# A third set of slots for the gathered rows of a graph attention kernel

## The reference

```python
def _gat_layer(x, src, dst, W_i, a_src_i, a_dst_i, b_i):
    h = (x @ W_i).reshape(n, H, C)              # 4 heads of 32 channels
    es = jnp.einsum('nhc,hc->nh', h, a_src_i)
    ed = jnp.einsum('nhc,hc->nh', h, a_dst_i)
    e = es[src] + ed[dst]
    e = jnp.where(e > 0, e, NEG_SLOPE * e)
    m = jax.ops.segment_max(e, dst, num_segments=n)
    p = jnp.exp(e - m[dst])
    denom = jax.ops.segment_sum(p, dst, num_segments=n)
    alpha = p / denom[dst]
    msg = alpha[:, :, None] * h[src]
    out = jax.ops.segment_sum(msg, dst, num_segments=n)
    return out.reshape(n, H * C) + b_i
```

## Time and profile before

| | us |
|---|---|
| median of 3 runs | 10176.32 |
| lowest and highest run | 10164.33, 10180.4 |
| span of the profiled execution | 10190.0 |
| POOL busy | 4949.5 (49%) |
| PE busy | 5634.0 (55%) |
| DVE busy | 5295.9 (52%) |
| ACT busy | 4630.7 (45%) |

### The profile page before, as it was taken

One profiled execution on the slowest core, in us unless ns is written; L12 is line 12 of the kernel. 1 busy time (PEld: TensorE's weight loads), 2 busy tenths in 40 slices (PEclk: granted clock), 3 DMA queues, 4 the chain that ended last, 5 costly groups with the idle time before them and its releaser, 6 DMA issues.

```text
span 10190.0 us, 128499 instructions
## 1 busy us (share of the span) xinstructions
PE 5634.0 (55%) x33883; PEld 4498.0 (44%) x33883; DVE 5295.9 (52%) x12476; ACT 4630.7 (45%) x8410; POOL 4949.5 (49%) x5153
## 2 busy tenths in 40 slices
PE   3999899735445454544454444545434444444446
PEld 2777566524444444443444444444423333333334
DVE  5888511335555555554555555555634444444445
ACT  2555200245555555553555555555434444444444
POOL 1000100356666666662566666666456666666660
PEclk9999899655555555555555555555555555555557
DMA  2333355133333333332333333333322222222221
GB/s 83 137 139 139 133 189 190 34 98 106 101 101 102 101 104 104 102 101 59 100 103 100 102 102 102 105 102 102 79 71 74 72 70 70 75 70 70 70 75 32
DMA packets 600497, 985.13 MB, mean 97 GB/s; under 512 B 330887, under 2 KB 454493, under 8 KB 560781
## 3 DMA queue, kind: packets, MB, share of 16 engines
q1 hardware_dynamic: 216924, 540.94, 15.6%
q0 software_dynamic: 163376, 356.21, 14.9%
q10 hardware_dynamic: 219648, 81.82, 3.0%
HBM read 755.78 MB, written 222.74 MB: 96 GB/s over the span
## 4 chain that ended last, share of the span: by engine, by line
PE 28%; DVE 21%; another core or an unknown queue 18%; DVEq 15%; issue 12%; POOL 3%; ACT 2%; DMA 1%; POOLq 0%; ACTq 0%; SPq 0%
PE bank L1038 12%; DVEq L1352 11%; DVE acc L1982 10%; PE bank L1264 6%; POOL arena L704 3%; DVE arena L1969 3%; PE bank L1062 2%; DVEq L1982 2%; DVE bank L1938 2%; PE bank L1192 2%; PE bank L1204 2%; DVEq L1974 1%; DVE arena L1940 1%; PE bank L1335 1%
## 5 line engine op out<-in xcount | busy, mean ns | idle before, releaser
L704 POOL DMA_INDIRECT arena<-row_table,staged_idx x4980 | 4712.4, 946 | 3140.3 <-issue 1777.7
L1264 PE MATMUL bank<-arena 128*128 128x136 f32 x9984 | 2508.6, 431 | 1638.0 <-issue 737.8
L1264 PEld LDWEIGHTS bank<-arena 128*128 128x128 f32 x9984 | 2218.6, 318 | 1813.3 <-issue 1795.4
L1982 DVE TENSOR_TENSOR acc<-acc,bank 128x136 f32 x4992 | 1476.7, 296 | 2271.3 <-remote 950.9
L861 ACT ACTIVATE pick_dist<-col,dst_local 128x128 bf16<-128x128 f32 x4992 | 1521.8, 388 | 442.9 <-remote 407.8
L1038 PE MATMUL bank<-arena 128*128 128x385 bf16 (+1 forms) x7448 | 1325.0, 327 | 36.4 <-DVE arena L1722 19.9
L813 ACT COPY x_mem<-bank 128x384 f32<-128x384 f32 x416 | 199.0, 478 | 1714.5 <-remote 1192.8
L1038 PEld LDWEIGHTS bank<-arena 128*128 128x128 bf16 x7448 | 702.0, 98 | 457.6 <-issue 21.5
L648 POOL TENSOR_TENSOR arena<-acc,node_stat 128x896 f32 x14 | 24.8, 1771 | 1672.9 <-POOLq L660 988.4
L1969 DVE TENSOR_TENSOR arena<-arena,bank 128x528 f32<-128x528 f32 x1248 | 832.3, 688 | 0.7
L1204 PE MATMUL bank<-ident,x_mem 96*128 96x96 f32 x1664 | 364.3, 374 | 764.0 <-DVE x_mem L1630 521.4
(11 more groups left out here) (371 smaller groups left out, 5508.6 us busy)
## 6 DMA issues: line engine op xcount, KB each, us to landing
arena<-dst_rows SPq DMA_DIRECT2D x156, 1024.0 KB
cell_rows<-arena SPq DMA_DIRECT2D x75, 1568.0 KB, 5.1
arena<-cell_rows SPq DMA_DIRECT2D x75, 1568.0 KB, 6.5
edge_stats<-x_mem ACTq DMA_DIRECT2D x416, 192.0 KB
arena<-row_table,staged_idx POOLq DMA_INDIRECT x4980
x_mem<-in_edge_attr SPq DMA_DIRECT2D x208, 192.0 KB
x_mem<-segment_flags SPq DMA_DIRECT2D x416, 96.0 KB
arena<-change_rows SPq DMA_DIRECT2D x312, 64.0 KB
```

What stands on the lines that cost most here:

```text
L704: pool.indirect_dma_start(gathered[:, at, :], None, table, bass.IndirectOffsetOnAxis(staged_idx[:, at:at + 1], 0)).then_inc(att_gathered[n ...
L1264: mm = pe.matmul(region(k)[:, 0:ROW], pick[:, k, :], gathered[:, b * GROUP + k, :], start=True, stop=True)
L1982: done = dve.tensor_tensor(row, row, region(m * BATCH + k), ALU.add)
```

## The change

A constant `SETS = 3` is new. The gathered rows get three sets of 32 slots. Two are the memory they had; the third is the last 32 of the 49 tiles of `H`, right before it in `arena`. Group g uses the set `(g + 1) % 3`. Groups 1, 4, ... 49 lie in `H`'s memory. POOL now waits for sums of group g - 3 and not at all for the first three groups of a layer; ACT stages three groups at the layer's start, and later, when the rows of group g + 1 have landed, those of group g + 4. After SP's last edge loads of a layer it waits for the sums of group 49 and loads tiles 17 to 48 of `H` back from the table; DVE waits for that load before it uses `H` at the layer's end. The two halves of `gathered` keep their other uses. The core of the diff:

```diff
+        OWN_KEPT = NT - GROUP
+        row_sets = arena[:, OWN_KEPT * ROW:(NT + 2 * GROUP) * ROW].rearrange("p (k w) -> p k w", w=ROW)
...
-        staged_idx = sb("staged_idx", [P, 2 * GROUP], I32)
+        staged_idx = sb("staged_idx", [P, SETS * GROUP], I32)
...
+        def row_set(g):
+            return (g + 1) % SETS
+        def set_rows(g):
+            first = (row_set(g) + 1) % SETS * GROUP
+            return row_sets[:, first:first + GROUP, :]
+        def rows_gathered(g):
+            return 16 * (g // SETS * GROUP + (LAST_REAL if g == NG - 1 else GROUP))
...
+                sp.wait_ge(att.summed, (n * NG + NG) * NBATCH)
+                sp.dma_start(H[:, OWN_KEPT:NT, :], table.rearrange("(t p) w -> p t w", p=P)[:, OWN_KEPT:NT, :]
+                             ).then_inc(n3.own_back, 16)
...
-                        pool.wait_ge(att.staged, n * (NG + 1) + it * 2 + b + 1)
-                            pool.wait_ge(att.summed, (n * NG + it * 2 + b) * NBATCH + (q + 1) * (ROUND // BATCH))
+                for g in range(NG):
+                    pool.wait_ge(att.staged, n * NG + g + 1)
+                    for q in range(RNG):
+                        if g >= SETS:
+                            pool.wait_ge(att.summed, (n * NG + g - SETS + 2) * NBATCH + (q + 1) * (ROUND // BATCH))
+                        pool.sem_inc(tick, 1)
+                        last = LAST_REAL if g == NG - 1 else GROUP
+                        for k in range(q * ROUND, min((q + 1) * ROUND, last)):
+                            at = row_set(g) * GROUP + k
+                            pool.indirect_dma_start(set_rows(g)[:, k, :], None, table,
+                                                    bass.IndirectOffsetOnAxis(staged_idx[:, at:at + 1], 0)
+                                                    ).then_inc(att_gathered[n][row_set(g)], 16)
...
+                def stage(g):
+                    c, slot = row_set(g), (g + SETS) * GROUP
+                    act.wait_ge(att_gathered[n][c], rows_gathered(g))
+                    nc.scalar.copy(staged_idx[:, c * GROUP:(c + 1) * GROUP],
+                                   src_of[:, slot:slot + GROUP]).then_inc(att.staged, 1)
...
-                    if ahead:
-                        stage(1 - b, it + b, it * (2 * GROUP) + (b + 1) * GROUP)
+                    if g + 1 + SETS < NG:
+                        stage(g + 1)
...
+                dve.wait_ge(n3.own_back, 16 * (n + 1))
                 dve.tensor_tensor(att_w[:, 0, :, :], H[:, :, AW:ROW], score_t, ALU.add)
```

More of the change, by code:

```diff
@@ L46 @@
 BATCH = 4
+SETS = 3
 SCAN_CHUNKS = 4
@@ L393, in build_graph_network @@
                           "log_scale scale_rows scale weighted used")
-        att_gathered = [[sem(f"att{n}_gathered{b}") for b in range(2)] for n in range(LAYERS)]
+        att_gathered = [[sem(f"att{n}_gathered{c}") for c in range(SETS)] for n in range(LAYERS)]
         cells_moved = [d0.moved0, d0.moved1, d0.moved2, d0.moved3]
@@ L693, in _ @@
                     pool.sem_inc(att.summed, 2 * NBATCH)
-                for it in range(PAIRS):
-                    for b in range(2):
-                        pool.wait_ge(att.staged, n * (NG + 1) + it * 2 + b + 1)
-                        for q in range(RNG):
-                            pool.wait_ge(att.summed, (n * NG + it * 2 + b) * NBATCH + (q + 1) * (ROUND // BATCH))
[L700 to L706, removed]
+                for g in range(NG):
[10 more added lines that the diff above has]
+                                                    ).then_inc(att_gathered[n][row_set(g)], 16)
                 if n == STATS_LAYERS - 1:
@@ L878, in _ @@
             for n in range(LAYERS):
-                for b in range(2):
-                    nc.scalar.copy(staged_idx[:, b * GROUP:(b + 1) * GROUP],
-                                   src_of[:, b * GROUP:(b + 1) * GROUP]).then_inc(att.staged, 1)
+                for g in range(SETS):
+                    c = row_set(g)
+                    nc.scalar.copy(staged_idx[:, c * GROUP:(c + 1) * GROUP],
+                                   src_of[:, g * GROUP:(g + 1) * GROUP]).then_inc(att.staged, 1)
                 if n == 0:
@@ L928, in _ @@
                     build_pick_t(n * NG + 2, part_no)
-                stage(0, 0, 0)
+                stage(0)
                 act_exps(n * NG, 0)
@@ L1263, in sum_batch @@
                     for k in range(m * BATCH, (m + 1) * BATCH):
-                        mm = pe.matmul(region(k)[:, 0:ROW], pick[:, k, :], gathered[:, b * GROUP + k, :],
+                        mm = pe.matmul(region(k)[:, 0:ROW], pick[:, k, :], set_rows(G - n * NG)[:, k, :],
                                        start=True, stop=True)
@@ L1888, in _, with score_edges @@
                 dve.memset(carry_b[:, :], FAR)
-                def group_rows(b):
-                    return gathered[:, b * GROUP:(b + 1) * GROUP, :]
-                def score_edges(head, b, use):
+                def score_edges(head):
+                    g = head - n * NG
                     dve.wait_ge(att.dst_scored, head + 1)
@@ L1949, in shift_scores @@
                                       ).then_inc(att.log_scale, 1)
-                    dve.tensor_tensor(group_rows(b)[:, :, AW:ROW].rearrange("p s h -> p h s"), back,
+                    dve.tensor_tensor(set_rows(head - n * NG)[:, :, AW:ROW].rearrange("p s h -> p h s"), back,
                                       last_edge[:, bass.ds(slot, GROUP)].unsqueeze(1)
@@ L1990, in dve_group @@
                     rescale(G, slot)
-                    weigh(G, b, 0)
-                    weigh(G, b, 1)
+                    weigh(G, 0)
+                    weigh(G, 1)
                     late = 0 if ahead else 3
```

22 lines of the change are left out of this document (9 added, 13 removed).

## The result

The kernel after takes 10220.4 us, the median of 4 runs (10214.9 to 10229.4); the kernel before beside it takes 10175.1 (10164.3 to 10180.4). The ratio is 1.0048, with a 95% interval of 1.0034 to 1.0062: slower by about half a per cent. The prediction was 10227 us, slower.

The account below looks back on a forecast made before the run. No engine full; POOL's 40 us a group plus pauses that let PE through set the period. Start +30 and end -13.2 a layer, three layers +50 on 10190.0, less 13.7: 10227 us; range 10060 to 10300, own range 10180 to 10280.

Parts of the forecast that it names:

- Start of a layer: First 96 gathers run unbroken, holding PE and DVE: first rescale later by +30 us in each layer.
- late instruction fetch: Alternative cause of slowed instructions at a layer's start: slow whatever POOL does, the +30 would go, sum 10136 us.
- The bounds of +25 and +40: Range for the first rescale's delay at each layer's start: at least +25 us, at most +40 if everything is held.
- End of a layer: Rows issued one group earlier, so one more group runs without gathers, 35.7 us against 48.9: -13.2 us per layer.
- Steady state: Middle of each layer: POOL fills all free sets, then waits as before; pauses stay, value 0.
- rival 3: POOL's pauses in every group go, as it issues a group further ahead: 8832 us, a third of it 9762; chance 0.06.
- Rival 4: Longer POOL runs hold PE longer in the steady state: +1 us a group, 10377 us; chance 0.10.
- Reload: SP's added load of H's tiles, one a layer, about 7.3 us, covered by the last groups: 0.
- Rival 2: Layer start not held, or made up within the first groups: 10136 us, with half the delay 10181; chance 0.14.

Follow-up runs that it names:

- first kind: Sessions, sets of runs made together on one chip, in which the kernel before took 10094 to 10188 us.
- the waits after 16: Kernel after, but POOL waits for sums after every 16 gathers, not 8, in the first layer's groups 35 to 51: period 55.5 us (after: 49.0).
- second kind: Sessions, sets of runs made together on one chip, in which the kernel before took 8713 to 8724 us.

## Why the prediction was right

Right in sign and size (10227 for 10220), and in the main by its own reasons, as far as the first kind of session goes.

**Start of a layer**, forecast +30: +30.6, +31.9, +31.1 (136.0 - 105.4, 135.3 - 103.4, 135.3 - 104.2), 93.6 in all for 90. The mechanism is shown by two edits, not only by the comparison: POOL stopped after 32 gathers gives 70.1 us, after 64 102.7, after 96 135. The other reading of the slow start, late instruction fetch, would have left it slow whatever POOL does; it falls with these. The Trainium skill (Runtime: NRT & Kernel Launch, Instruction fetch mechanics) has the cost of fetching mostly hidden, and the trace agrees: in after the two instruction queues take 0.1% each of the DMA engines' time. Nor is it fetch that the gathers delay. These are all DMA packets of after from 4759 to 4865 us, by queue, and none is of an instruction queue, though PE and DVE stood still from 4792.3 and went on at 4827.93:

```profile
q0 software_dynamic: 2728, 5.95, 24.9%
q1 hardware_dynamic: 144, 1.05, 2.4%
```

One reading of the rows was wrong. The prediction has the 32 score matmuls take "some 60 us" under gathers and concludes that those of group 1 can't be done there. They took 25.6 us (4756.5 to 4782.1), and the rest of that wait is the 36 us behind them, in which neither PE nor DVE ran anything; and in after group 1's were done in 28 us, most of them under the run. Of the 33.3 us by which the way from group 0's scores to the rescale grew (26.0 to 59.3), 21.7 are those matmuls and 11.6 the rest, mostly the exchanges. The bounds of +25 and +40 took this work to lie behind the run. It lay mostly under it, slowed, and the slowing then went on for 12 us behind it. So the rescale still came between the bounds, and that the term's size is so close is partly luck.

**End of a layer**, forecast -13.2: the last two periods sum to 70.3 us in the second layer where they were 85.1. In the three layers that is -14.9, -14.8 and -17.0, -46.7 in all for -39.6. The prediction read its 35.7 and 48.9 from the second layer, where one group more runs free, as forecast; in the first and third both of the last two groups got shorter.

**Steady state**, forecast 0: first rescale to the 50th went from 2402.1, 2408.6 and 2359.6 us to 2397.8, 2398.7 and 2355.4, -18.4 in all or 0.13 us a group. DVE's 165.5 us of waiting for rows are gone, and at least nine tenths of that bought nothing: slack, as the third layer's period had said. Even the 18.4 may not be a gain. They come from one execution of each kernel, and the kernel before alone is 19 to 27 us a layer apart, first rescale to the 50th, in its traces of two sessions of the first kind. The pauses stayed, 9.1 us a group for 9.3, so rival 3 failed. The Trainium skill (Perfetto Trace Analysis, Identifying Performance Opportunities) says that such bubbles can come from too little memory for the next tile, the buffer count; here they did not. Rival 4, longer runs in the steady state, didn't come either, though the waits after 16 show that its price is real and above my 1 us a group: 6.5, had the runs got longer.

**Reload**, forecast 0 with 7.3 us for the transfer: 10.4 us to landing, 20 us early. Without it the time is the same (1.0001), though that was asked in the second kind only, where POOL is the bound. The kernel with three sets that waits two groups back, which was to show in one number that reload and staging cost nothing, ran in the second kind only too.

Sum of the parts: 93.6 - 46.7 - 18.4 = +28.5; the spans differ by 25.2, the rest lies behind the last layer (188.2 us from its last rescale to the end before, 184.9 after). I had +50 (3 x 16.8 = 50.4); the 21.9 between them are 18.4 of steady state and 7.1 of ends, less 3.6 of starts. That the median hit within 7 us is partly luck: the pair of medians has 45 where the pair of profiles has 25, and which of the two is the better measure of the parts wasn't settled.

**What the argument did not have**: it took the slowed instructions as part of the kernel's time in any session. In the second kind they don't exist, the first rescale comes at 58.9 us in after, and the change has no effect (0.9997). Rival 2's "the start isn't held" is true there, but its gain (10136) isn't, since POOL's 40 us a group hide everything. And rival 3's 8832 us is nearly the time of both kernels there: the bubbles do go, but not by the buffer.

## What to carry over

Before giving a producer more buffers, ask what its unbroken run does to the engines it feeds: here one more set meant 32 more gathers without a pause at each layer's start, +31 us, for 15 to 17 us at its end, and moving them only moved the cost. Waits for data that vanish are no gain where another wait sets the period; 165 us of them were worth 18 at most. And look in the trace whether an edit that allows shorter runs gives shorter runs: here it did not. Where a kernel's time rests on one engine slowing others, measure in more than one session: a change worth +0.5% in one kind was nothing in the other.

## What the hardware showed

The same kernel before took 10094 to 10188 us in three sessions and 8713 to 8724 in four, with runs within 0.2% of each other in each session that had more than one. Outside the stretches with gathers the two kinds agree: the traces of after are 34.9 us apart at the first gather of the first layer (2038.2 and 2003.3), and 31.4 of these arise in the first 200 us, where POOL gathers too. In the layers the difference is the slowing of the other engines during runs of gathers; the gathers cost 0.944 us in both kinds and start 1.25 apart. It isn't TensorE's clock: from the first gather of the first layer to the first rescale the granted clock is 0.50 of full speed, the 1.2 GHz level, in both traces of after, and that way takes 136 us in one and 59 in the other. By which path a gather holds the other engines isn't shown; the rows tell that the time passes between the operations of an engine and not in them, and that the slowing outlasts the run by 4.5 us after 32 gathers and 12 after 96. What makes the kind isn't known. It may not be the chip: one chip number turned up with a kernel before of 10094 and again with 8716.

A drain of POOL's queue behind gathers held back the next gather by 2.2 us after every gather, rising to 3.4 after every 32, where I had expected 1; a single one behind hundreds of gathers held it back by 9.1 us, another by 5.1.
